# A graph attention block on one core: pair sums merged in the accumulators' bank, the carry row fetched from the stored sums, exponents moved to the front of ScalarE's order, node pieces regrouped, a loop of two turns

## The chip, the cores and the metric

The kernel runs on one core of a Trainium2 chip. The core has five engines that work side by side, each through its own list of instructions: TensorE (PE, with PEld for the weight loads), VectorE (DVE), ScalarE (ACT), GpSimd (POOL) and SyncE (SP, which here only issues DMAs). They meet through semaphores. The metric is the device time in microseconds of one execution.

## The reference

One attention layer over a graph of 6250 nodes and 100,000 edges sorted by destination, then a feed-forward part, residuals and a last layer norm. Cut to what matters here:

```python
q, k, v = feat @ W.T + b            # 6250 x 256 each, 8 heads of 32
score = clip(sum_d(q[dst] * k[src]) / sqrt(32), -10, 10)     # 100000 x 8
ex    = exp(score - segment_max(score, dst)[dst])
den   = segment_sum(ex, dst)
wv    = segment_sum(ex / den[dst] * v[src], dst)
x1    = feat + wv @ Wp.T + bp
h     = gelu(layernorm(x1) * ln_g + ln_b @ W1.T + b1) @ W2.T + b2   # 256 -> 1024 -> 256
out   = layernorm(feat + x1 + h)
```

The clip bounds the exponent, so the kernel leaves the maximum out and divides the sums at the end.

## The kernel before, in words

First the rows k|v of all nodes are computed and stored in DRAM (`kv_rows`), and the first q rows too. Then come the edges. 128 edges make a tile, 4 tiles a batch, 2 batches a pair, 8 batches a turn. There are 196 batches, 98 pairs and 25 turns (0 to 24). Every engine runs its own list over the turns through `turns` (L279): turns 0 to 4 and the last are written out, turns 5 to 23 are a loop (Fori) of one turn. Inside a turn, position i goes from 0 to 7, and n = 8 turn + i is the batch that VectorE begins there.

What a batch costs, engine by engine:

- GpSimd gathers 4 tiles of k|v rows by an indirect DMA each (L313), into one of 8 slots of `kv`. It waits until VectorE has used the slot, and every half turn for a new load of source indices `src_sb` (two buffers, loaded by `load_sources`, L519 of the queue).
- TensorE selects the q rows of the batch's edges from a window of 32 rows for each tile (`q_rows`, L776, into `quad`).
- VectorE multiplies them with k (`products`, L1299), sums by head (`scores`, L1306), clips (L1313), and multiplies v with the exponent of the batch two earlier (`weight`, L1321, into `ev`). Once a pair it makes the one-hot rows (L1287).
- ScalarE makes two exponents of each batch (`exponent`, L1008 into bank 5, L1009 into `ev`), and for each pair the transposed one-hots (L994, L999).
- TensorE sums the weighted rows of a batch by destination into 4 windows of bank 4 (`sums`, L785).

After the second batch of a pair, ScalarE copies bank 4 into `staged` (`stage`, L1017). TensorE then puts the four windows in their places with `place` (L758), and adds the carry: the last node of the pair before may go on in this one, so a second matmul (L762) takes the one row of the previous `acc_sb` that `carry_sel` selects. Both write bank 5, the bank that also holds the exponents. `merge` therefore waits for the exponents, and `weight` of every odd batch waits until `copy_sums` (L1023) has read the result. SyncE stores the 80 rows of sums (`store_sums`, L540) to `agg_rows`.

Nodes ride along in blocks of 256, in `node_steps`. In turn t, block t-1 is loaded (`load_node_sums`, L439), divided by its denominators (`normalise`, i = 3), projected (i = 4, 5), added to x (`residual`, i = 6) and normed (`norm_roots`, i = 7). Block t-2 goes through the feed-forward part: four pieces `ffn1` at i = 1 to 4 with their biases on ScalarE at i = 2 to 5, one Gelu over 128x2048 at i = 5 (L387), and `ffn2` in pieces of 3, 3 and 2 of its 8 slices at i = 6, 7 and 0 of the next turn. Gelu and Exp lie in different tables of ScalarE, so each Gelu has a table load on either side. A unit of q rows is projected each turn as well.

The order on each engine is the order in which the code is written. SyncE's list is in order too: a wait in it holds up every DMA that is written behind it.

An integer check at the start (`check_edges`, `set_flag`) tests that each tile's destinations fit its window, and otherwise a slow general path follows at the end.

## Time and profile before

| | us |
|---|---|
| median of 3 runs | 1251.4 (1251.23 to 1254.77) |
| the profiled execution's own time | 1251.61 |
| its span | 1249.8 |
| first gather issued | 94.84 |
| last gather issued | 1157.58 |
| products of the first and the last batch begin | 103.27, 1175.79 |

The page gives each engine's busy time as a share of the span. PE and DVE both show over 80%. A share does not say which of two such engines sets the pace; the waits and the order in time do. The timeline shows what an engine does at each moment, and in square brackets how long it sat idle before, and what ended that.

### The profile page before, as it was taken

How to read it: one execution, taken by the hardware profiler on the slowest of the kernel's cores; microseconds unless marked ns; L12 is line 12 of the kernel's file. 1: busy time of each engine (PE TensorE's matmuls, PEld its weight loads, DVE VectorE, ACT ScalarE, POOL GpSimd, SP SyncE). 2: the span in 40 equal slices, each digit the busy share in tenths (PEclk: the TensorE clock that was granted, in tenths of full speed). 3: DMA queues.
4: the chain of work that ended last, by engine and by line, in shares of the span. 5: the costliest groups of instructions: out<-in, count | busy, mean ns of one | idle time of the engine just before them, and what ended most of it. 6: DMA issues, size and time to landing. Idle time of an engine off the chain costs nothing.

```text
span 1249.8 us, 24882 instructions
## 1 busy us (share of the span) xinstructions
PE 1032.2 (83%) x6118; PEld 670.4 (54%) x6118; DVE 1014.9 (81%) x1779; ACT 525.6 (42%) x1353; POOL 746.1 (60%) x802
## 2 busy tenths in 40 slices
PE   7893568888988978888888888789889788888887
PEld 6671235555645645555555555456556455555565
DVE  4875788888978978898898888889889888888733
ACT  2221225345444544535445444454444445354332
POOL 0007777777676676767767667666766767667000
PEclk9995588989988988998998988998889889889989
DMA  7777898888888887887887888888788878878210
GB/s 239 247 257 230 284 316 276 251 275 264 254 247 247 265 243 228 268 259 236 258 254 242 256 242 252 255 255 251 238 254 261 246 244 266 248 241 255 69 30 27
DMA packets 158513, 297.71 MB, mean 238 GB/s; under 512 B 34216, under 2 KB 94726, under 8 KB 158471
## 3 DMA queue, kind: packets, MB, share of 16 engines
q0 software_dynamic: 62720, 205.57, 53.4%
q1 hardware_dynamic: 95750, 91.66, 23.2%
q8 instruction: 17, 0.28, 0.1%
q14 instruction: 26, 0.20, 0.1%
HBM read 261.99 MB, written 35.13 MB: 238 GB/s over the span
## 4 chain that ended last, share of the span: by engine, by line
PE 39%; DVE 24%; issue 22%; ACT 8%; POOL 3%; DMA 2%; DVEq 1%; ACTq 1%; POOLq 0%
PE bank L374 10%; DVE score L1306 7%; PE quad L729 5%; DVE ev L1321 5%; PE bank L394 5%; PE bank L758 4%; PE bank L785 4%; POOL kv L313 3%; ACT hid L382 3%; PE bank L762 3%; DVE prod L1299 2%; ACT L1008 2%; PE bank L796 2%; PE quad L776 2%; DVE stats L404 2%
## 5 line engine op out<-in xcount | busy, mean ns | idle before, releaser
L313 POOL DMA_INDIRECT kv<-kv_rows,src_sb x784 | 743.2, 948 | 411.6 <-issue 224.3
L1321 DVE TENSOR_TENSOR ev<-kv,bank 128x1024 f32<-128x1024 f32 x196 | 238.3, 1216 | 93.7 <-ACT ev L1009 71.7
L1299 DVE TENSOR_TENSOR prod<-kv,quad 128x1024 f32<-128x1024 f32 x196 | 238.7, 1218 | 41.5 <-DMA kv<-kv_rows,src_sb 24.1
L1306 DVE TENSOR_REDUCE score<-prod 128x32 f32<-128x1024 f32 x196 | 237.4, 1211 | 0.0
L776 PE MATMUL quad<-qwin,onehotT 32*128 32x256 f32 x1568 | 148.3, 448 | 90.5 <-DVE onehot L1287 73.4
L785 PE MATMUL bank<-ev,onehot 128*32 128x264 f32 x1568 | 144.6, 444 | 86.4 <-DVE ev L1321 85.4
L394 PE MATMUL bank<-w_sb,hid 128*128 128x256 f32 x736 | 202.8, 431 | 0.0
L374 PE MATMUL bank<-hT,w_sb 128*128 128x256 f32 x728 | 176.9, 386 | 0.0
L394 PEld LDWEIGHTS bank<-w_sb,hid 128*128 128x128 f32 x736 | 153.2, 216 | 39.6 <-issue 17.0
L776 PEld LDWEIGHTS quad<-qwin,onehotT 32*128 32x128 f32 x1568 | 66.6, 193 | 164.4 <-issue 110.0
L374 PEld LDWEIGHTS bank<-hT,w_sb 128*128 128x128 f32 x728 | 132.9, 190 | 35.2 <-issue 19.2
L382 ACT ACTIVATE hid<-bank,b_sb 128x256 f32<-128x256 f32 x182 | 76.3, 470 | 119.5 <-PE bank L374 119.5
L785 PEld LDWEIGHTS bank<-ev,onehot 128*32 128x32 f32 x1568 | 32.5, 114 | 161.8 <-DVE ev L1321 120.2
L1023 ACT ACTIVATE acc_sb<-bank 128x264 f32<-128x264 f32 x98 | 38.2, 390 | 187.2 <-PE bank L762 185.1
L758 PE MATMUL bank<-staged,place 128*128 128x264 f32 x196 | 88.1, 539 | 11.4 <-ACT ev L1009 9.0
L1008 ACT ACTIVATE bank<-clipped 128x32 f32<-128x32 f32 x196 | 38.4, 196 | 135.3 <-issue 84.5
L1017 ACT ACTIVATE staged<-bank 128x264 f32<-128x264 f32 x98 | 37.8, 386 | 121.8 <-PE bank L785 118.2
L729 PE MATMUL quad<-wqkv_sb,xT_parts 128*128 128x512 f32 x300 | 71.9, 400 | 13.4 <-DVE xT_parts L1175 13.4
L762 PE MATMUL bank<-acc_sb,carry_sel 128*128 128x264 f32 x194 | 74.1, 471 | 0.0
L758 PEld LDWEIGHTS bank<-staged,place 128*128 128x128 f32 x196 | 36.3, 231 | 69.5 <-ACT ev L1009 50.7
L729 PEld LDWEIGHTS quad<-wqkv_sb,xT_parts 128*128 128x128 f32 x300 | 57.5, 193 | 26.1 <-DVE wqkv_sb L1270 9.2
L999 ACT ACTIVATE onehotT<-distance,one_col 128x256 f32<-128x256 f32 x98 | 49.8, 508 | 9.4
(109 smaller groups left out, 1088.4 us busy)
## 6 DMA issues: line engine op xcount, KB each, us to landing
dst_rows<-edge_dstT SPq DMA_DIRECT2D x200, 64.0 KB
kv_rows<-kv_out SPq DMA_DIRECT2D x25, 512.0 KB, 3.4
...
kv<-kv_rows,src_sb POOLq DMA_INDIRECT x784
...
xT_sb<-xT SPq DMA_DIRECT2D x25, 256.0 KB, 3.8
...
xq_sb<-xT SPq DMA_DIRECT2D x24, 256.0 KB
```

The source lines that it names most:

```text
L313: return nc.gpsimd.indirect_dma_start(out=rows, out_offset=None, in_=kv_dram, in_offset=bass.IndirectOffsetOnAxis(ap=index, axis=0))
L374: last = nc.tensor.matmul(bank[:, j * SB:(j + 1) * SB], w1_sb[:, k * HIDDEN + f * P:k * HIDDEN + (f + 1) * P], hT[:, k], start=(k == 0), s ...
L382: last = nc.scalar.activation(hid[:, f], bank[:, j * SB:(j + 1) * SB], ACT.Identity, bias=b1_sb[:, f:f + 1])
L394: last = nc.tensor.matmul(bank[:, a * C:(a + 1) * C], hid[:, f, a * P:(a + 1) * P], w2_sb[:, f * C:(f + 1) * C], start=False, stop=(a == 1 ...
L729: last = nc.tensor.matmul(rows, lhsT, rhs, start=(n == 0), stop=(n == len(passes) - 1))
L758: last = nc.tensor.matmul(bank5[:, 0:ACC], place[:], staged[:, slot % 2], start=True, stop=not exists(p - 1, PAIRS))
L762: last = nc.tensor.matmul(bank5[:, 0:ACC], carry_sel[:, slot % 2], acc_sb[:, (slot + 3) % 4], start=False, stop=True)
L776: last = nc.tensor.matmul(quad[:, i, 0:C], onehotT[rows, slot // 2, cols], qwin[rows, slot // 2], start=True, stop=True)
L785: last = nc.tensor.matmul(bank4[WIN * i:WIN * (i + 1), 0:ACC], onehot[:, slot // 2, TILES * (slot % 2) + i, :], ev[:, slot % 4, i], start= ...
L1299: nc.vector.tensor_tensor(prod[:, slot % 2].rearrange("p (i c) -> p i c", c=C), kv[:, slot, :, 0:C], quad[:, :, 0:C], ALU.mult).then_inc(s ...
L1306: nc.vector.tensor_reduce(score[:, slot % 2], prod[:, slot % 2].rearrange("p (h d) -> p h d", d=HD), AX.X, ALU.add).then_inc(s_score, 1)
L1321: nc.vector.tensor_tensor(ev[:, slot % 4, :, 0:C].rearrange("p i (h d) -> p i h d", d=HD), kv[:, slot, :, C:2 * C].rearrange("p i (h d) -> ...
```

## The change

Seven things, all in one diff:

1. `merge` writes bank 4, the accumulators' own bank, with one matmul, `place` on `staged`. The second matmul, `carry_sel`, `carry_all` and `select_carry` are gone. The sums of the next pair wait for `copy_sums` (before: for `stage`).
2. The carry row comes in through row 127 of `staged`. A new step `load_carry(p)` on SyncE waits until the sums of pair p-1 are stored (all earlier ones too), reads the pair's base from `bases_sb` and fetches that one row of `agg_rows`. `merge(p)` waits for it. Row 127 of `place` leads to row 0; so a window's last row is given up, and the check asks for one row less (and the fourth window starts at 41).
3. The exponents and the counting row `iota` live alone in bank 5. `weight` no longer waits for `copy_sums`; the one-hots wait for the exponents of the batch before last.
4. On ScalarE `exponent` and `copy_sums` stand first in each position; the Gelu moves from i = 5 to i = 4, behind the exponent.
5. Node pieces move: `ffn1` to i = 0 to 3, `ffn2` to i = 5, 6, 7 in pieces of 3, 2 and 3 slices, the transpose of h to i = 7, `residual` to i = 5, `norm_roots` to i = 6, `output` to 0, `residual_twice` to 1. On VectorE they stand ahead of `scores`, on TensorE ahead of `sums` (but at i = 5).
6. Source indices have 4 buffers and are loaded two turns ahead. The unit of x for q is loaded half a turn earlier. 3 gathers of the empty tail are left out (781 instead of 784).
7. The loop body holds two turns: 6 turns in front, 9 rounds of two, 1 behind.

Two places of the order. First ScalarE, in turn 2, the first with a Gelu; `bank5<-clipped` and `ev<-clipped` are the two exponents of a batch, `hid<-hid` is the Gelu. Before:

```order
L1023 ACTIVATE acc_sb<-bank5 128x264
L1026 ACTIVATE carry_sel<-carry_all 128x1
L336 ACTIVATE wvT<-bank6 128x512
L382 ACTIVATE hid<-bank7,b1_sb 128x256 x2
L387 ACT_TABLE_LOAD
L387 ACTIVATE hid<-hid 128x2048
L1008 ACT_TABLE_LOAD
L1008 ACTIVATE bank5<-clipped 128x32
L1009 ACTIVATE ev<-clipped 128x4x8
```

And now:

```order
L1003 ACTIVATE bank5<-clipped 128x32
L1004 ACTIVATE ev<-clipped 128x4x8
L1018 ACTIVATE acc_sb<-bank4 128x264
L395 ACT_TABLE_LOAD
L395 ACTIVATE hid<-hid 128x2048
L989 ACTIVATE distance<-dst_rows,minus_start 128x256
L994 ACTIVATE onehotT<-distance,one_col 128x256
L1003 ACT_TABLE_LOAD
L1003 ACTIVATE bank5<-clipped 128x32
L1004 ACTIVATE ev<-clipped 128x4x8
```

The Gelu has gone ahead by one position, and an exponent and the copy of the sums stand right in front of it; the transposed one-hots, which before came behind the next exponent, now lie between the Gelu and that exponent.

Second SyncE, written-out turn 4, positions 1 and 2: the store of the sums, the output rows of an older block, a pair's q windows, the load of a block's sums. `TENSOR_LOAD bases_sb` reads a pair's base. Before:

```order
L540 DMA agg_rows<-acc_sb 80x264
L447 DMA out<-y_out 106x256
L499 TENSOR_LOAD bases_sb
L499 ISA x2
L506 ISA
L506 DMA qwin<-q_rows 32x256
...
L439 DMA agg_in<-agg_rows 128x2x264
```

And now, in turn 5, which is written out too:

```order
L555 DMA agg_rows<-acc_sb 80x264
L455 DMA out<-y_out 128x2x256
L508 TENSOR_LOAD bases_sb
L508 ISA x2
L547 ISA
L547 DMA staged<-agg_rows 1x264
L508 TENSOR_LOAD bases_sb
L508 ISA x2
L515 ISA
L515 DMA qwin<-q_rows 32x256
...
L447 DMA agg_in<-agg_rows 128x2x264
```

Between the store and the load of the block's sums there is now another base and another DMA, and the first of them waits for the store to have landed.

```diff
-EX_COL = ACC
-IOTA_COL = C
+EX_COL = 0
+IOTA_COL = 2 * TILES * H
...
         def turns(eng, body):
-            for turn in range(min(5, TURNS - 1)):
-                body(turn)
-            if TURNS > 6:
-                with eng.Fori(5, TURNS - 1) as turn:
-                    body(turn)
-            body(TURNS - 1)
+            looped = max(TURNS - 7, 0) // 2
+            first = 6 if looped else TURNS - 1
+            for turn in range(first):
+                body(turn, turn // 2, turn % 2)
+            if looped:
+                with eng.Fori(3, 3 + looped) as r:
+                    body(2 * r, r, 0)
+                    body(2 * r + 1, r, 1)
+            for turn in range(first + 2 * looped, TURNS):
+                body(turn, turn // 2, turn % 2)
...
-        F2_PARTS = ((0, 1, 2), (3, 4, 5), (6, 7))
+        F2_PARTS = ((0, 1, 2), (3, 4), (5, 6, 7))
...
-                    sp.wait_ge(s_kv[4 * t + b], 64 * (h // 2) if isinstance(h, int) else 64 * h[0])
+                    sp.wait_ge(s_kv[4 * t + b], 64 * (turn + 1))
                 sp.sem_inc(s_gate_sp, 1)
-                col = h * HALF if isinstance(h, int) else h[1]
-                sp.dma_start(src_sb[:, t], edge_src[:, bass.ds(col, HALF)]).then_inc(s_src[t], 16)
+                buffer = 2 * parity + t
+                sp.dma_start(src_sb[:, buffer], edge_src[:, bass.ds((2 * turn + (4 + t)) * HALF, HALF)])\
+                    .then_inc(s_src[buffer], 16)
...
+            def load_carry(p, slot):
+                sp.wait_ge(s_aggst, 16 * p)
+                base = pair_base(p)
+                sp.dma_start(staged[P - 1:P, slot % 2], agg_dram[bass.ds(base, 1), :]).then_inc(s_carry, 16)
 
...
+                    done = 4 * turn + i // 2 - 2
+                    if i == 0 and exists(turn - 1, Q_UNITS - EARLY_Q):
+                        sp.wait_ge(f_qst, 16 * turn)
+                    elif i == 0 and isinstance(turn, int) and turn > 0:
                         sp.wait_ge(f_qst, 16 * (Q_UNITS - EARLY_Q))
-                    if i % 2 == 1 and exists(4 * turn + i // 2 - 2, PAIRS):
-                        store_sums(4 * turn + i // 2 - 2, (i // 2 + 2) % 4)
+                    if i % 2 == 0 and exists(done, PAIRS) and exists(done - 1, PAIRS):
+                        load_carry(done, (i // 2 + 2) % 4)
+                    if i % 2 == 1 and exists(done, PAIRS):
+                        store_sums(done, (i // 2 + 2) % 4)
...
                     if i == 4 and exists(turn, Q_UNITS - EARLY_Q):
                         store_q_unit(turn)
+                    if i == 4 and exists(turn + 1, Q_UNITS - EARLY_Q):
+                        load_q_unit(turn + 1)
...
-                pe.wait_ge(s_exp, min(2 * p + 4, BATCHES) if isinstance(p, int) else 2 * p + 4)
-                last = nc.tensor.matmul(bank5[:, 0:ACC], place[:], staged[:, slot % 2], start=True,
-                                        stop=not exists(p - 1, PAIRS))
                 if exists(p - 1, PAIRS):
-                    pe.wait_ge(s_csel, p)
-                    last = nc.tensor.matmul(bank5[:, 0:ACC], carry_sel[:, slot % 2], acc_sb[:, (slot + 3) % 4],
-                                            start=False, stop=True)
-                last.then_inc(s_mrg, 1)
+                    pe.wait_ge(s_carry, 16 * p)
+                nc.tensor.matmul(bank4[:, 0:ACC], place[:], staged[:, slot % 2], start=True, stop=True)\
+                    .then_inc(s_mrg, 1)
...
-                    if slot % 2 == 1:
-                        pe.wait_ge(s_oh, p + 1)
...
                 if slot % 2 == 0 and exists(p - 1, PAIRS):
-                    pe.wait_ge(s_stc, p)
+                    pe.wait_ge(s_accc, p)
...
+                    if i % 2 == 0 and exists(4 * turn + i // 2 - 2, PAIRS):
+                        merge(4 * turn + i // 2 - 2, (i // 2 + 2) % 4)
+                    if i != 5:
+                        node_steps(turn, i)
                     if exists(n - 2, BATCHES):
                         sums(n - 2, (i - 2) % SLOTS, 4 * turn + (i - 2) // 2)
-                    if i % 2 == 0 and exists(4 * turn + i // 2 - 2, PAIRS):
-                        merge(4 * turn + i // 2 - 2, (i // 2 + 2) % 4)
-                    node_steps(turn, i)
+                    if i == 5:
+                        node_steps(turn, i)
...
+                if i <= 3 and exists(turn - 2, SUPERBLOCKS):
+                    ffn1(turn - 2, i)
+                if i == 1 and exists(turn, Q_UNITS - EARLY_Q):
+                    project_q(turn)
+                if i == 3 and exists(turn - 1, SUPERBLOCKS):
+                    transpose_wv(turn - 1)
                 if i == 4 and exists(turn - 1, SUPERBLOCKS):
-                    transpose_wv(turn - 1)
-                if i == 5 and exists(turn - 1, SUPERBLOCKS):
                     project_out(turn - 1)
-                if i == 0 and exists(turn - 2, SUPERBLOCKS):
-                    transpose_h(turn - 2)
-                if 1 <= i <= 4 and exists(turn - 2, SUPERBLOCKS):
-                    ffn1(turn - 2, i - 1)
-                if i in (6, 7) and exists(turn - 2, SUPERBLOCKS):
-                    ffn2(turn - 2, i - 6)
-                if i == 0 and exists(turn - 3, SUPERBLOCKS):
-                    ffn2(turn - 3, 2)
-                if i == 2 and exists(turn, Q_UNITS - EARLY_Q):
-                    project_q(turn)
+                if i == 7 and not ends and exists(turn - 1, SUPERBLOCKS):
+                    transpose_h(turn - 1)
+                if i >= 5 and not ends and exists(turn - 2, SUPERBLOCKS):
+                    ffn2(turn - 2, i - 5)
...
-                nc.scalar.activation(staged[:, slot % 2], bank4[:, 0:ACC], ACT.Copy).then_inc(s_stc, 1)
+                nc.scalar.activation(staged[0:P - 1, slot % 2], bank4[0:P - 1, 0:ACC], ACT.Copy).then_inc(s_stc, 1)
...
-                nc.scalar.activation(acc_sb[:, slot], bank5[:, 0:ACC], ACT.Copy).then_inc(s_accc, 1)
-
-            def select_carry(p, slot):
-                nc.scalar.activation(carry_sel[:, slot % 2, 0:1], carry_all[:, bass.ds(p, 1)], ACT.Copy)\
-                    .then_inc(s_csel, 1)
+                nc.scalar.activation(acc_sb[:, slot], bank4[:, 0:ACC], ACT.Copy).then_inc(s_accc, 1)
...
-                if i == 5 and exists(turn - 1, SUPERBLOCKS):
+                if i <= 3 and exists(turn - 2, SUPERBLOCKS):
+                    ffn1_bias(turn - 2, i)
+                if i == 3 and exists(turn - 1, SUPERBLOCKS):
                     copy_wv(turn - 1)
-                if i == 0 and exists(turn - 2, SUPERBLOCKS):
-                    norm_out(turn - 2)
-                if i == 1 and exists(turn - 2, SUPERBLOCKS):
-                    scale_h(turn - 2)
-                if 2 <= i <= 5 and exists(turn - 2, SUPERBLOCKS):
-                    ffn1_bias(turn - 2, i - 2)
-                if i == 5 and exists(turn - 2, SUPERBLOCKS):
+                if i == 4 and not ends and exists(turn - 2, SUPERBLOCKS):
                     gelu(turn - 2)
...
+                if i == 7 and not ends and exists(turn - 1, SUPERBLOCKS):
+                    scale_h(turn - 1)
+                if i == 7 and exists(turn - 3, SUPERBLOCKS):
+                    norm_out(turn - 1)
...
                     n = SLOTS * turn + i
+                    if exists(n - 1, BATCHES):
+                        exponent(n - 1, (i - 1) % SLOTS)
+                    if isinstance(turn, int) and n == BATCHES:
+                        gelu(SUPERBLOCKS - 3, range(FC // 2))
+                    done = 4 * turn + i // 2 - 2
+                    if i % 2 == 0 and exists(done, PAIRS):
+                        copy_sums(done, (i // 2 + 2) % 4)
                     node_steps(turn, i)
+                    if i % 2 == 1 and exists(done + 1, PAIRS):
+                        stage(done + 1, (i // 2 + 3) % 4)
+                    if isinstance(turn, int) and n == BATCHES + 1:
+                        gelu(SUPERBLOCKS - 3, range(FC // 2, FC))
                     if i % 2 == 0 and exists(4 * turn + i // 2 + 2, PAIRS):
                         transposed_onehots(4 * turn + i // 2 + 2, (i // 2 + 2) % 4, turn + i // 4 + 1)
-                    if exists(n - 1, BATCHES):
-                        exponent(n - 1, (i - 1) % SLOTS)
-                    p = 4 * turn + i // 2 - 2
-                    if i % 2 == 1 and exists(p + 1, PAIRS):
-                        stage(p + 1, (i // 2 + 3) % 4)
-                    if i % 2 == 0 and exists(p, PAIRS):
-                        copy_sums(p, (i // 2 + 2) % 4)
-                        if exists(p + 1, PAIRS):
-                            select_carry(p + 1, (i // 2 + 3) % 4)
+                    if i == 6 and exists(turn - 1, SUPERBLOCKS):
+                        norm_h(turn - 1)
...
+                if exists(p - 1, PAIRS):
+                    dve.wait_ge(s_exp, 2 * p - 1)
                 if exists(p - 4, PAIRS):
                     dve.wait_ge(s_part, 2 * p - 6)
...
-                    dve.wait_ge(s_accc, p)
                 first = EX_COL + slot % 2 * TILES * H
...
                 inverse_roots(norm_tiles(c), norm_step(c, [2]))
 
             def node_steps(turn, i):
-                if i == 3 and exists(turn, Q_UNITS - EARLY_Q):
+                if i == 0 and exists(turn - 3, SUPERBLOCKS):
+                    output(turn - 3)
+                if i == 1 and exists(turn - 2, SUPERBLOCKS):
+                    residual_twice(turn - 2)
+                if i == 2 and exists(turn, Q_UNITS - EARLY_Q):
                     q_bias(turn)
+                if i == 3 and exists(turn - 1, SUPERBLOCKS):
+                    normalise(turn - 1)
                 if i == 5 and isinstance(turn, int) and turn == 0:
                     split_biases()
-                if i == 3 and exists(turn - 1, SUPERBLOCKS):
-                    normalise(turn - 1)
-                if i == 6 and exists(turn - 1, SUPERBLOCKS):
+                if i == 5 and exists(turn - 1, SUPERBLOCKS):
                     residual(turn - 1)
                     norm_moments(turn - 1)
-                if i == 7 and exists(turn - 1, SUPERBLOCKS):
+                if i == 6 and exists(turn - 1, SUPERBLOCKS):
                     norm_roots(turn - 1)
-                if i == 1 and exists(turn - 3, SUPERBLOCKS):
-                    output(turn - 3)
-                if i == 2 and exists(turn - 2, SUPERBLOCKS):
-                    residual_twice(turn - 2)
-
-            def edges(turn):
+
+            def edges(turn, r, parity):
                 for i in range(SLOTS):
                     n = SLOTS * turn + i
+                    if exists(n - 1, BATCHES):
+                        clip(n - 1, (i - 1) % SLOTS)
                     if exists(n, BATCHES):
                         products(n, i, turn)
                     if i % 2 == 0 and exists(4 * turn + i // 2, PAIRS):
                         onehots(4 * turn + i // 2, i // 2)
                     if exists(n - 2, BATCHES):
-                        weight(n - 2, (i - 2) % SLOTS, 4 * turn + (i - 2) // 2)
+                        weight(n - 2, (i - 2) % SLOTS)
+                    node_steps(turn, i)
                     if exists(n, BATCHES):
                         scores(n, i)
-                    if exists(n, BATCHES):
-                        clip(n, i)
-                    node_steps(turn, i)
-
-            nc.vector.memset(carry_sel[:], 0.0)
+
+            nc.vector.memset(staged[:], 0.0)
             dve.wait_ge(s_iota, 1)
```

## Rows read from the trace of the kernel before

**Rows 1.** The page, part 1: busy time, share of the span, instructions.

```profile
PE 1032.2 (83%) x6118; PEld 670.4 (54%) x6118; DVE 1014.9 (81%) x1779; ACT 525.6 (42%) x1353; POOL 746.1 (60%) x802
```

**Rows 2.** Busy time by stretch (stretch, length, engines, clock, DMA share, GB/s).

```profile
142.00:182.00 40.00, 24.30 (x153) 12.25 (x149) 31.73 (x44) 10.09 (x35) 30.26 (x33) 0.74 0.96 313
...
586.00:1140.00 554.00, 478.67 (x2947) 304.41 (x2949) 481.60 (x808) 260.09 (x680) 378.49 (x400) 0.91 0.82 251
```

**Rows 3.** Waits of VectorE, 182 to 1162 us (total, times, longest).

```profile
DVE ev L1321 <- ACT ev L1009: 71.7, 22, 3.4
DVE ev L1321 <- ACT acc_sb L1023: 13.7, 13, 1.4
```

**Rows 4.** TensorE in order of time: after idling, busy, and near the end.

```profile
631.59 0.88 PE L776 MATMUL quad<-qwin,onehotT 32*128 32x256 f32 x8 [2.55 <-DVE onehot L1287]
...
633.75 1.25 PE L758 MATMUL bank<-staged,place 128*128 128x264 f32 x2
...
1174.57 0.71 PE L758 MATMUL bank<-staged,place 128*128 128x264 f32 x2
...
1196.67 9.81 PE L394 MATMUL quad<-w_sb,hid 128*128 128x256 f32 x32
```

**Rows 5.** VectorE in order of time (start, length, row, idle before).

```profile
187.53 1.22 DVE L1299 TENSOR_TENSOR prod<-kv,quad 128x1024 f32<-128x1024 f32 x1
...
1118.48 1.22 DVE L1299 TENSOR_TENSOR prod<-kv,quad 128x1024 f32<-128x1024 f32 x1 [0.70 <-DVE root L418]
...
1137.06 1.21 DVE L1299 TENSOR_TENSOR prod<-kv,quad 128x1024 f32<-128x1024 f32 x1
...
1138.53 1.21 DVE L1321 TENSOR_TENSOR ev<-kv,bank 128x1024 f32<-128x1024 f32 x1
...
1141.07 1.22 DVE L1299 TENSOR_TENSOR prod<-kv,quad 128x1024 f32<-128x1024 f32 x1
...
1149.60 1.22 DVE L1321 TENSOR_TENSOR ev<-kv,bank 128x1024 f32<-128x1024 f32 x1 [3.24 <-ACT ev L1009]
...
1161.72 1.22 DVE L1299 TENSOR_TENSOR prod<-kv,quad 128x1024 f32<-128x1024 f32 x1 [0.30 <-DVE root L418]
```

**Rows 6.** ScalarE in order of time, around one Gelu.

```profile
612.48 1.28 ACT L387 ACT_TABLE_LOAD   x1
613.77 1.91 ACT L387 ACTIVATE hid<-hid 128x2048 f32<-128x2048 f32 x1
615.70 1.28 ACT L1008 ACT_TABLE_LOAD   x1
```

**Rows 7.** Groups by line (busy, mean ns, idle before): one node piece.

```profile
L400 DVE TENSOR_TENSOR z<-bank,xx 128x512 f32<-128x512 f32 x23 | 15.9, 691 | 9.9 <-PE bank L394 9.0
```

**Rows 8.** GpSimd's 1st and 60th gather, and one after a load of indices.

```profile
94.84 1.10 POOL L313 DMA_INDIRECT kv<-kv_rows,src_sb  x1 [91.04 <-DMA kv_rows<-kv_out]
...
168.75 0.95 POOL L313 DMA_INDIRECT kv<-kv_rows,src_sb  x1 [0.30 <-DVE ev L1321]
...
606.63 0.94 POOL L313 DMA_INDIRECT kv<-kv_rows,src_sb  x1 [2.65 <-DMA src_sb<-edge_src]
```

**Rows 9.** SyncE's queue in order of time, sums stored and fetched.

```profile
194.88 0.33 SPq L540 DMA_DIRECT2D agg_rows<-acc_sb  x1
...
198.29 0.40 SPq L439 DMA_DIRECT2D agg_in<-agg_rows  x1
...
592.36 0.34 SPq L540 DMA_DIRECT2D agg_rows<-acc_sb  x1
...
594.66 1.90 SPq L506 DMA_DIRECT2D qwin<-q_rows  x4
597.03 0.39 SPq L439 DMA_DIRECT2D agg_in<-agg_rows  x1
```

**Rows 10.** DMA issues (KB each, median us to landing).

```profile
wp_sb<-wpT SPq DMA_DIRECT2D x1, 256.0 KB, 4.3
```

**Rows 11.** SyncE's queue: the load of indices before that gather.

```profile
601.80 0.37 SPq L519 DMA_DIRECT2D src_sb<-edge_src  x1
```

164 lines of the change are left out of this document (65 added, 99 removed).

## The prediction

> **What bounds the kernel now.** I read the page's busy shares first, then the stretches, the waits of VectorE, and one turn of it in order of time. The shares leave two candidates, TensorE with 83% and VectorE with 81% [rows 1]. Between 586 and 1140 us VectorE is busy 481.6 of 554 us, and the DMA engines 0.82 of the time [rows 2]. What decides is who waits for whom. From 182 to 1162 us VectorE waits for no matmul worth naming, but 71.7 us (22 times) for exponents and 13.7 us (13 times) for the copy of a pair's sums [rows 3]. TensorE, with its larger share, waits for VectorE's one-hots and products instead, as in the 2.55 us of [rows 4]. So VectorE sets the pace, and its own idle time is what can be won.
>
> The unit is a turn. Turn 2 begins on VectorE at 187.53, turn 24 at 1161.72: 974.2 us for 22 turns, 44.28 us each [rows 5]. In each one the wait for exponents stands once, 3.24 us [rows 5]. Its cause is the block on ScalarE of a table load (1.28), the Gelu (1.91) and a load back (1.28), 4.5 us in one piece, with the next exponent behind it [rows 6].
>
> **The change part by part.**
>
> *Gelu.* It now stands right behind an exponent. I lay out turn time from VectorE's rows. A position with one-hots takes 4.0 us (1137.06 to 1141.07), without them about 3.7, each 0.69 us node piece adds about 0.6 as such rows overlap [rows 5, 7]. From the start of position 4, its `weight` ends at +2.6; ScalarE then has exponents 0.5, copy of sums 0.4, load, Gelu and back 4.5 [rows 6], one-hots about 1.0 in between, exponents 0.5: ready at +9.5. VectorE wants it at position 6 behind the products. Position 4 takes 4.0, position 5 with residual and moments some 6.5, products 1.1: +11.6. Cover of 2 us remains, so the wait goes entirely: -71.7 us. If the cover were gone, each turn would pay what is missing.
>
> ScalarE's table loads are weighed against a rule. The row shows Gelu starting 1.29 us after its load began, and no pause [rows 6]. The Trainium skill (ScalarE: Activation LUTs, What ACT_TABLE_LOAD costs) gives about 2.66 us for a switch, the load and a drain. By that the block would last 7.2 us, the cover would be short by some 0.5 us, and 22 turns would pay 11 us. The trace disagrees, and I go by its rows.
>
> *Merge in bank 4.* `weight` no longer waits for `copy_sums`: -13.7 us [rows 3]. The carry matmul and a small ScalarE instruction go, on engines that wait for VectorE: 0. The sums of the next pair now wait for the copy, about 1 us later than for `stage`; they stand behind a node piece anyway, and TensorE has time: 0.
>
> *Loop of two turns.* Behind a jump back VectorE idles 0.70 us, behind the same row without a jump 0.30 [rows 5]. 18 jumps become 8: -4.0 us.
>
> *Four index buffers.* GpSimd's pace is 73.91 us for 59 steps, 1.25 us per gather, 40.1 us for the 32 of a turn [rows 8]. Today it adds a wait such as 2.65 us twice a turn, because the indices come late; that goes. As GpSimd was ahead of VectorE, it is worth nothing by itself. Without it GpSimd would be the bound at once, since VectorE's turn becomes 44.28 - (71.7 + 13.7 + 4.0) / 22 = 40.2 us. The two are now level. The bytes of a turn, 251 GB/s for 44.28 us, took 35.5 us at the 313 GB/s that stood once [rows 2]; the DMA engines can carry it, at about 0.9 of their time.
>
> *The carry row.* This is the price. Before, SyncE issued the store of the sums at 592.36, the q windows from 594.66 and the load of a block's sums at 597.03, 4.67 us later [rows 9]. Now it first waits until the store has landed (S), reads a base (about 1.0 us, my estimate from the 1.96 us between the store's end and the windows, which also hold an output store), issues the carry row (0.35), and then does windows and load as before (3.4 with their base): S + 4.7. S was never waited for. From above it is at most the 3.4 us between store and load at 194.88 and 198.29, since that load waited for it too [rows 9]; from below nothing excludes 1 us. I take 2.5, nearer to the row. So the block's sums go out 7.2 us behind the store, 2.5 later than now. Their landing (A, 264 KB): 256 KB took 4.3 us to land [rows 10], and 8 KB of indices 4.83 us from issue to the gather behind them [rows 8, 11]. I take 4.5, with ends of 3 and 6 as the DMA engines are busier.
>
> When does VectorE want them? `normalise` now stands at position 3 behind `weight`: 4.6 + 4.3 + 4.6 + 2.3 = 15.8 us into the turn. And when is the store issued? TensorE's position 7 holds q rows, the transposes of h, 12 matmuls of `ffn2` (3 slices where it had 2) and only then the sums; with `stage`, merge, copy and a base read the store comes at about 4.8 us into the turn. But at position 6 VectorE spends 2.7 us in roots, TensorE idles some 3 us, and after such a gap its clock is at the lower level: after 2.55 us idle `place` took 1.25 us against 0.71 [rows 4]. Then it is 6.5 us. The sums are there at 4.8 or 6.5, + 7.2 + 4.5 = 16.5 or 18.2. VectorE waits 0.7 or 2.4 us per turn. I take 1.4, 22 times 1.4 = 31 us given back.
>
> The same S and the landing of the carry row (L) also make a round from merge to merge: merge, copy and signals 1.1, base and issue 1.1, S, base 0.9, L: 3.1 + S + L. With S = 2.5 and L = 3.5 (one row of 1 KB, below the 4.83) it is 9.1 us, four times a turn 36.4, and 1.2 more where SyncE is still busy with other issues: 37.6, beneath 40.2. It is hidden, but not by much.
>
> *Regrouped pieces.* TensorE's list fits under VectorE's in each position at full clock, `residual` finds its projection finished: 0, except for what stands above.
>
> *End.* The last store needs the carry too, which takes back what the earlier last `weight` wins. But block 22 has its Gelu in two halves inside turn 24, so the 9.81 us of `ffn2` that began at 1196.67 [rows 4] begin some 5 us earlier relative to the last products, and all that follows hangs on them: -5 us. Between 0 and -9.
>
> *Sum*, against the profiled execution's own time of 1251.6, which is 0.2 above the median: 1251.6 - 71.7 - 13.7 - 4.0 + 31 - 5 = 1188 us.
>
> **Rivals.**
>
> 1. *No wait for the block's sums.* If S is 2 and A is 3.5, and TensorE keeps its clock, they arrive at 4.8 + 6.7 + 3.5 = 15.0, before 15.8. Then the turn is 40.2 us and the time 1157. For it speaks that nothing before ever waited for this load; against it, that the load moves 2.5 us back while its reader moves forward. The Trainium skill (DMA: Bandwidth & Descriptors, Anatomy of one DMA — SWDGE (gpsimd) path) puts a DMA at a fixed 2.0 us or so plus its bytes over 436 GB/s, which would make S 2.2 and A 2.6, and the result this rival. The 4.83 us for 8 KB here are more than twice that [rows 8, 11], so the rule gets only a share.
>
> 2. *The carry's round becomes the bound, and the kernel slower.* Each pair must wait for a store and a load through DRAM. With S at its upper bound of 3.4 and L at 4.8 the round is 11.3 us, the turn 4 x 11.3 + 1.2 = 46.4, and the time 1251.6 + 22 x 2.1 - 5 = 1293. It decides from S + L = 7.7 on, where the turn passes 44.28; from 7.0 on it exceeds my turn of 41.6. For it: busier DMA engines (0.96 in the stretch of [rows 2]). Against it: a longer turn relieves the DMA engines, and S had its bound at 0.86.
>
> 3. *The general path.* The check asks for one row less, and the fourth window begins at 41. From the reference's own edges the largest place in a window is 29 where 30 are allowed, the smallest 0, and a pair spans at most 70 of 79 nodes. So this one is out.
>
> **How the numbers follow.** My case, a turn of 41.6 us with 1 us to either side, gets 0.63 and reaches from 1166 to 1210. Rival 1 gets 0.22, near 1157. The carry's round gets 0.12: half of it between 1210 and 1248, half slower. The rest is for what I have not seen. What a measurement here can tell from no change is about 0.3%, 4 us. Faster by more than that 0.92, within it 0.02, slower 0.06. The range that should hold the time 8 times in 10 is 1155 to 1224.
>
> **What would show it.** Right: no wait of VectorE for exponents behind a Gelu; none for the copy of the sums; GpSimd's waits for indices gone, and waits for `ev` in their place; a wait of `den` or `wv` for the load of sums, 1 to 2 us once a turn; the last gather near 1090. Rival 1 shows as no such wait and turns of 40.2. Rival 2 shows as waits of the merge for the DMA of `staged`, and behind them waits of VectorE's products for q rows, or of the one-hots for exponents. The forecast fails if S and A lie far from 2.5 and 4.5, or if TensorE falls behind at its lower clock in position 7, which I priced only through the store.

## The result, and the profile after

The changed kernel takes 1259.1 us (median of 7 runs, 1257.3 to 1265.4) against 1252.2 for the kernel before, run beside it (7 runs, 1251.2 to 1255.3): ratio 1.0058, 95% interval 1.0037 to 1.008. It is slower by 0.6%, where 1188 was forecast. The profiled execution took 1265.4 us, its span is 1263.5.

Part 1 of the page and the stretch 586 to 1140 us, the answers to [rows 1, 2]:

```profile
PE 1024.3 (81%) x5924; PEld 655.2 (52%) x5924; DVE 1015.2 (80%) x1777; ACT 518.5 (41%) x1257; POOL 744.0 (59%) x801
```

```profile
586.00:1140.00 554.00, 464.35 (x2755) 290.73 (x2752) 471.78 (x804) 251.57 (x613) 370.27 (x392) 0.86 0.79 245
```

VectorE has as much work as before and does less of it in the stretch; TensorE's granted clock fell from 0.91 to 0.86. VectorE's waits from 182 to 1162 us, as [rows 3] (total, times, longest):

```profile
DVE den L326 <- DMA agg_in<-agg_rows: 77.1, 22, 5.5
DVE x L360 <- PE bank L354: 29.7, 17, 1.9
DVE z L408 <- PE bank L402: 10.2, 14, 2.0
```

The waits for Gelu and for the copy of the sums are gone, 85.4 us. In their place stand 77.1 us for the block's sums, where 31 were forecast, and 29.7 for the projection, where nothing was; 10.2 more stand in front of `z`. One turn shows how. VectorE (start, length, row, idle before; `prod` at 636.76 begins the turn):

```profile
636.76 1.22 DVE L1281 TENSOR_TENSOR prod<-kv,quad 128x1024 f32<-128x1024 f32 x1
...
651.54 1.21 DVE L1301 TENSOR_TENSOR ev<-kv,bank 128x1024 f32<-128x1024 f32 x1
658.28 0.17 DVE L326 TENSOR_SCALAR den<-agg_in 128x16 f32<-128x16 f32 x1 [5.52 <-DMA agg_in<-agg_rows]
```

and SyncE's queue in the same turn, as [rows 9]:

```profile
640.14 1.33 SPq L515 DMA_DIRECT2D qwin<-q_rows  x3
641.74 1.82 SPq L472 DMA_DIRECT2D dst_rows<-edge_dstT  x4
644.55 0.34 SPq L555 DMA_DIRECT2D agg_rows<-acc_sb  x1
645.44 0.42 SPq L455 DMA_DIRECT2D out<-y_out  x1
649.33 0.30 SPq L547 DMA_DIRECT2D staged<-agg_rows  x1
650.79 1.86 SPq L515 DMA_DIRECT2D qwin<-q_rows  x4
653.13 0.40 SPq L447 DMA_DIRECT2D agg_in<-agg_rows  x1
```

The sums that are stored at 644.55 had been copied by ScalarE at 641.36 already:

```profile
641.36 0.39 ACT L1018 ACTIVATE acc_sb<-bank 128x264 f32<-128x264 f32 x1 [0.46 <-PE bank L778]
```

Read the queue backwards. VectorE wants the sums at 652.76. They were asked for at 653.13. Ahead of that stand four windows and a base read (from 649.63 on), the carry row, and the wait for the store to land (from 645.86 to some 648.5). And the store itself is 2.8 us behind the end of the copy, because SyncE was still issuing destination rows.

This last part is not typical. I went through the 20 turns between 190 and 1100 us by the same rows. The store goes out 0.9 to 3.5 us behind the end of the copy, in the middle (median) 1.2, where it was 1.0 before the change. On average the store stands 6.6 us into the turn, the sums are asked for 8.2 us later (7.6 to 8.8), land 5.0 later still, and VectorE, which wants them at 16.4, waits 3.5. So in an ordinary turn it is the wait for the landed store, with what stands behind it in the queue, that makes the sums late. SyncE has no busy share on the page. The chain that ended last, by engine, names it with 15%, and DMAs with 22%:

```profile
PE 29%; DMA 22%; DVE 19%; SPq 15%; issue 12%; POOL 1%; ACT 1%; DVEq 0%; ACTq 0%; POOLq 0%
```

What the prediction said of the other engines is there. ScalarE has the Gelu between its table loads as in [rows 6], and no one waits for the exponents behind it; GpSimd waits for VectorE's `ev` over the whole span, not for indices:

```profile
1164.61 1.28 ACT L395 ACT_TABLE_LOAD   x1
1165.90 1.91 ACT L395 ACTIVATE hid<-hid 128x2048 f32<-128x2048 f32 x1
...
1168.86 1.28 ACT L1003 ACT_TABLE_LOAD   x1
```

```profile
POOL kv L321 <- DVE ev L1301: 112.9, 83, 3.6
```

### The profile page after: what moved, and what is told of

Same layout as the page of the kernel before. It is cut to its first block, busy times and chain, and to the rows that moved or that the text cites. A ratio compares the mean times of both kernels' runs of the same rounds, so it can differ in the third digit from the quotient of the medians.

```text
span 1263.5 us, 24619 instructions
## 1 busy us (share of the span) xinstructions
PE 1024.3 (81%) x5924; PEld 655.2 (52%) x5924; DVE 1015.2 (80%) x1777; ACT 518.5 (41%) x1257; POOL 744.0 (59%) x801
## 4 chain that ended last, share of the span: by engine, by line
PE 29%; DMA 22%; DVE 19%; SPq 15%; issue 12%; POOL 1%; ACT 1%; DVEq 0%; ACTq 0%; POOLq 0%
DMA agg_rows<-acc_sb 12%; DMA agg_in<-agg_rows 6%; SPq L508 5%; PE bank L402 5%; DVE score L1288 5%; PE bank L354 5%; SPq L515 5%; PE quad L748 5%; PE quad L789 4%; DVE prod L1281 3%; PE bank L778 3%; DVE ev L1301 2%; SPq L472 2%; DMA staged<-agg_rows 2%; DVE stats L412 1%
## 5 line engine op out<-in xcount | busy, mean ns | idle before, releaser
L789 PE MATMUL quad<-qwin,onehotT 32*128 32x256 f32 x1568 | 163.4, 490 | 118.0 <-DVE prod L1281 112.6
L402 PE MATMUL bank<-w_sb,hid 128*128 128x256 f32 x736 | 200.2, 428 | 0.0
L789 PEld LDWEIGHTS quad<-qwin,onehotT 32*128 32x128 f32 x1568 | 71.8, 213 | 216.8 <-issue 122.6
L382 PE MATMUL bank<-hT,w_sb 128*128 128x256 f32 x736 | 182.2, 392 | 0.4 <-ACT hid L390 0.4
L402 PEld LDWEIGHTS bank<-w_sb,hid 128*128 128x128 f32 x736 | 157.3, 219 | 30.5 <-issue 5.6
L382 PEld LDWEIGHTS bank<-hT,w_sb 128*128 128x128 f32 x736 | 139.0, 194 | 34.0 <-ACT hid L390 10.3
L390 ACT ACTIVATE hid<-bank,b_sb 128x256 f32<-128x256 f32 x184 | 77.1, 470 | 111.9 <-PE bank L382 111.9
L778 PE MATMUL bank<-staged,place 128*128 128x264 f32 x196 | 84.5, 519 | 44.2 <-DMA staged<-agg_rows 43.4
L354 PE MATMUL bank<-wp_sb,wvT 128*128 128x256 f32 x200 | 82.5, 585 | 0.0
L1012 ACT ACTIVATE staged<-bank 127x264 f32<-127x264 f32 x98 | 38.1, 388 | 107.4 <-PE bank L798 107.2
L326 DVE TENSOR_SCALAR den<-agg_in 128x16 f32<-128x16 f32 x25 | 4.8, 192 | 88.0 <-DMA agg_in<-agg_rows 88.0
## 6 DMA issues: line engine op xcount, KB each, us to landing
agg_rows<-acc_sb SPq DMA_DIRECT2D x98, 82.5 KB
```

The lines of the kernel that those rows point to most:

```text
L354: last = nc.tensor.matmul(bank6[:, a * C:(a + 1) * C], wvT[:, (a * KC + k) * P:(a * KC + k + 1) * P], wp_sb[:, k * C:(k + 1) * C], start=F ...
L382: last = nc.tensor.matmul(bank[:, j * SB:(j + 1) * SB], w1_sb[:, k * HIDDEN + f * P:k * HIDDEN + (f + 1) * P], hT[:, k], start=(k == 0), s ...
L390: last = nc.scalar.activation(hid[:, f], bank[:, j * SB:(j + 1) * SB], ACT.Identity, bias=b1_sb[:, f:f + 1])
L402: last = nc.tensor.matmul(bank[:, a * C:(a + 1) * C], hid[:, f, a * P:(a + 1) * P], w2_sb[:, f * C:(f + 1) * C], start=False, stop=(a == 1 ...
L778: nc.tensor.matmul(bank4[:, 0:ACC], place[:], staged[:, slot % 2], start=True, stop=True)\
L789: last = nc.tensor.matmul(quad[:, i, 0:C], onehotT[rows, slot // 2, cols], qwin[rows, slot // 2], start=True, stop=True)
```

## How I compare the kernels

For each kernel I took the stretch 190 to 1100 us, the length of a turn there (first to last `z` row on VectorE over the turns between), SyncE's waits and the sum of all of VectorE's waits. SyncE's own time is what its waits leave over. For the changed kernel: 20 rows of `z` from 238.2 to 1094.5, so 45.07 us a turn and 20.19 turns in 910 us; its two waits are

```profile
SPq L507 <- DMA agg_rows<-acc_sb: 194.6, 72, 5.5
SPq L552 <- ACT acc_sb L1018: 28.8, 28, 3.7
```

so 9.6 and 1.4 us a turn, and 34.0 are its own. In us, per turn but for the first column:

| kernel | median | turn | SyncE's own | waits for stores | waits for copies | VectorE idle | turn less idle |
|---|---|---|---|---|---|---|---|
| before | 1252.4 | 44.41 | 27.4 | 0.0 | 17.0 | 5.0 | 39.4 |
| changed | 1259.1 | 45.07 | 34.0 | 9.6 | 1.4 | 5.6 | 39.5 |
| e1 sums first | 1228.0 | 43.17 | 33.7 | 9.2 | 0.3 | 3.7 | 39.4 |
| e2 no round | 1264.6 | 45.44 | 33.6 | 10.1 | 1.7 | 6.1 | 39.3 |
| e3 carry by matmul | 1149.3 | 40.26 | 28.3 | 0.1 | 11.8 | 0.9 | 39.4 |
| e5 sums first, no round | 1223.6 | 43.42 | 33.6 | 9.8 | 0.0 | 4.1 | 39.3 |
| e7 windows ahead | 1246.9 | 44.21 | 33.9 | 1.2 | 9.1 | 4.7 | 39.6 |
| e8 bases ahead too | 1201.6 | 42.03 | 34.0 | 0.7 | 7.2 | 2.5 | 39.5 |
| e9 exponent late | 1248.4 | 44.18 | 29.1 | 0.0 | 15.0 | 4.6 | 39.5 |
| e10 wait only | 1186.8 | 41.69 | 27.4 | 10.1 | 4.1 | 2.4 | 39.3 |

The last column is 39.3 to 39.6 in every row: VectorE's own work in a turn is the same in all, and every difference in the turn is its idle time. The columns in the middle show what SyncE does with the turn; what VectorE waits for is told with each run.

## The experiments

**e1, the block's sums first.** In SyncE's `edges`:

```diff
+                    if i == 2 and exists(turn - 1, SUPERBLOCKS):
+                        load_node_sums(turn - 1)
                     if i % 2 == 0 and exists(4 * turn + i // 2 + 2, PAIRS):
                         load_q_windows(4 * turn + i // 2 + 2, (i // 2 + 2) % 4)
...
-                    if i == 2 and exists(turn - 1, SUPERBLOCKS):
-                        load_node_sums(turn - 1)
```

> The changed kernel with one order turned round on SyncE: in each turn the load of the finished block's sums goes out right behind the carry's load, ahead of the four q windows of the same position. Theory A (the block's sums come late because the carry's wait for the store and the q windows stand ahead of them on SyncE, and the rest follows from that wait): in the changed kernel the last window issue stands 1.5 to 3.8 us behind the carry's load and ahead of the sums, so the sums go out about 3 us earlier; VectorE's wait before L326 falls from 3.5 us a turn to under 1, the wait before L360 from 1.8 to under 1, the turn from 45.1 us to 41 to 42, the time to 1160 to 1190 (1175). Theory B (the carry's round of store, load, merge and copy sets the turn): the round is as long as before, the waits move elsewhere, 1255 to 1262. Theory C (the loop of two turns or the regrouped node pieces make the turn longer by themselves): the wait before L326 goes but another takes its place, over 1240.

Measured 1228.0 (1222.0 to 1230.6), ratio to before 0.9816 [0.9789, 0.9843]. Neither number. The wait for the sums fell from 3.5 to 1.1 us a turn, but the turn only by 1.9, for TensorE's list now waits for the carry, 134.8 us where it was 30.6 in the changed kernel (all in 190 to 1100 us):

```profile
PE bank L778 <- DMA staged<-agg_rows: 134.8, 63, 5.0
PE quad L789 <- DVE prod L1281: 22.5, 33, 2.6
```

A pair's round of SyncE in this kernel:

```profile
605.56 0.36 SPq L555 DMA_DIRECT2D agg_rows<-acc_sb  x1
610.54 0.28 SPq L547 DMA_DIRECT2D staged<-agg_rows  x1
612.33 2.26 SPq L515 DMA_DIRECT2D qwin<-q_rows  x4
615.51 0.34 SPq L555 DMA_DIRECT2D agg_rows<-acc_sb  x1
```

The merge ran at 612.54, 2.0 us behind the issue of the row. One round is 9.95 us, the next 11.2 (with destination rows in it), then 9.6.

**e2, the round cut at the merge.**

```diff
-                sp.dma_start(staged[P - 1:P, slot % 2], agg_dram[bass.ds(base, 1), :]).then_inc(s_carry, 16)
+                sp.dma_start(carry_row[P - 1:P, slot % 2], agg_dram[bass.ds(base, 1), :]).then_inc(s_carry, 16)
...
-                if exists(p - 1, PAIRS):
-                    pe.wait_ge(s_carry, 16 * p)
```

> The changed kernel with the carry row loaded into a buffer of its own that nobody reads, and the merge without a wait for it (the sums of a node shared by two pairs are left incomplete; the last row of the staged tile stays zero). SyncE issues and waits exactly as before. Theory A: SyncE's queue is what it was, so the block's sums stay late: 1250 to 1262, with the same 3 us wait before L326. Theory B: the round is cut at the merge, the pairs no longer follow each other through DRAM: 1160 to 1185. Theory C: as A.

1264.6 (1257.7 to 1268.4), ratio 1.0081 [1.0047, 1.0114], for a kernel that leaves the carry out. The round by itself is not what the changed kernel waits for: the rival of a carry round as the bound falls for it.

**e3, the carry as before, all else of the change.**

```diff
-                if exists(p - 1, PAIRS):
-                    pe.wait_ge(s_carry, 16 * p)
-                nc.tensor.matmul(bank4[:, 0:ACC], place[:], staged[:, slot % 2], start=True, stop=True)\
-                    .then_inc(s_mrg, 1)
+                last = nc.tensor.matmul(bank4[:, 0:ACC], place[:], staged[:, slot % 2], start=True,
+                                        stop=not exists(p - 1, PAIRS))
+                if exists(p - 1, PAIRS):
+                    pe.wait_ge(s_csel, p)
+                    last = nc.tensor.matmul(bank4[:, 0:ACC], carry_sel[:, slot % 2], acc_sb[:, (slot + 3) % 4],
+                                            start=False, stop=True)
+                last.then_inc(s_mrg, 1)
```

with `carry_all`, `select_carry` back and `load_carry` gone.

> The changed kernel with the carry as the kernel before has it (selection column and a second matmul from the copied sums, now into bank 4), and no carry load on SyncE; all else of the change stays. Theory A: no wait for a landed store stands ahead of the q windows and the block's sums but the one that the sums themselves need; the sums go out 4.7 us behind the store as before the change, the wait before L326 is 1.4 us or less, the turn 41 to 42 us, the time 1160 to 1190. Theory B: also 1160 to 1190. Theory C: stays over 1240, since loop and regrouping are still there. ScalarE has 97 more copies of a column, some 0.3 us each, beside VectorE's work.

1149.3 (1146.2 to 1150.8), ratio 0.9172 [0.9146, 0.9198]: 8.3% faster than before, and 110 us under the changed kernel. The turn is 40.26 us, the 40.2 that the prediction had worked out for a VectorE that waits for nothing. Its stretch 586 to 1100, and what is left of the wait for the sums:

```profile
586.00:1100.00 514.00, 457.83 (x2994) 301.10 (x2994) 491.46 (x839) 264.76 (x693) 372.24 (x392) 0.96 0.85 267
```

```profile
DVE den L328 <- DMA agg_in<-agg_rows: 0.9, 3, 0.4
```

The queue in one turn of it: 4.5 us from the store to the sums, as before the change, with no wait between them, since the windows' issues fill the time in which the store lands.

```profile
640.58 0.34 SPq L552 DMA_DIRECT2D agg_rows<-acc_sb  x1
641.35 0.41 SPq L457 DMA_DIRECT2D out<-y_out  x1
642.76 1.89 SPq L517 DMA_DIRECT2D qwin<-q_rows  x4
645.08 0.39 SPq L449 DMA_DIRECT2D agg_in<-agg_rows  x1
```

`den` ran at 650.08, 5.0 us later. A load of the sums took 5.15 us in the turn above, and 4.73 in the one before it (608.30 to 613.03), so nearly nothing was to spare. The store stands 6.6 us into the turn on average here, as in the changed kernel; only the way from it to the sums is shorter.

**e4, the loop alone**: the kernel before with 6 turns written out, 9 rounds of two, and the last.

> The kernel before with nothing changed but the loop: six turns written out, nine rounds of two turns, the last turn. The prediction's term: ten loop jumps fewer at 0.4 us, minus 4.0 us: 1248 (1245 to 1251). Theory C (a body of two turns costs by itself): 1256 or more.

1247.0 (12 runs, 1243.2 to 1252.4), ratio 0.9975 [0.9959, 0.9991]: -3.1 us by the ratio, -5.4 by the medians. The term of -4.0 holds.

**e5, e1 and e2 together.**

> The changed kernel with the sums' load right behind the carry's load and with the carry loaded into a buffer that nobody reads (the sums of a node shared by two pairs are left incomplete). Singly, the first edit took the turn from 45.1 to 43.2 us and the second left it (45.4). Theory D (two waits lie one over the other: the late sums, and under them the carry's round of 10 to 11 us a pair): with both gone the turn is VectorE's own 40.3 to 41 us, the time 1149 to 1170. Theory E (what costs is that SyncE stands still for 5 us in each pair, whoever reads the carry): little is won over the 1228 of the sums-first kernel, 1210 to 1230.

1223.6 (1222.6 to 1230.4), ratio 0.9782 [0.9744, 0.982]. Theory D falls, E holds. This kernel leaves the carry out too. Although nobody reads the carry and the sums go out right behind it, VectorE still waits 49.2 us for them. SyncE has one wait left in the stretch, and none for a copy:

```profile
SPq L508 <- DMA agg_rows<-acc_sb: 206.0, 76, 5.1
```

Its own 33.6 us and 9.8 of standing still are 43.4, the whole turn. When it gets to a store, the copy has long been made: the store goes out 5.2 us behind it (median of all stores in the stretch), where that is 1.0 in the kernel before and in e3, and 1.5 in the changed kernel. That is a bound, of an engine whose rows have no busy share on the page. It lies at 43.4 us, so beneath the 45.07 of the changed kernel, and shows once the sums go out earlier.

**e7 and e8, the fetched carry with a better queue.** e7 is e1 with the windows issued ahead of the wait for the store; e8 also reads the pair's base ahead of the waits:

```diff
+                    if i % 2 == 0 and exists(4 * turn + i // 2 + 2, PAIRS):
+                        load_q_windows(4 * turn + i // 2 + 2, (i // 2 + 2) % 4)
                     if i % 2 == 0 and exists(done, PAIRS) and exists(done - 1, PAIRS):
                         load_carry(done, (i // 2 + 2) % 4)
...
+                base = pair_base(p)
                 sp.wait_ge(s_aggst, 16 * p)
-                base = pair_base(p)
```

> The changed kernel (its carry still fetched and used) with SyncE's order at each even position: q windows, then the wait for the store, the carry's load, then the block's sums. In the sums-first kernel a pair's round reads 605.56 store, 610.54 carry, 612.54 merge, 615.51 next store: 9.95 us, of which the last 3.0 hold the merge, the copy and the four windows with their base that SyncE must issue first (612.33 to 614.59). Theory D with SyncE's issues as part of the round: the windows go out while the store is under way, the next store follows the copy, about 1.3 us earlier; the round is 8.6 us, four of them 34.6, below VectorE's 40.3: turn 40.3 to 42, time 1150 to 1190. Theory F (store and load themselves are the round, the windows are beside it): 1220 to 1230 as the sums-first kernel.

> As the kernel with the windows ahead, and the pair's first row is read into its register before the waits of the carry's load and of the store, not behind them. By the gap of 0.7 to 0.8 us from a wait's end to an issue behind a register read, the round gets 1.4 us shorter: where the round still is the bound that is up to 5.6 us a turn, and the time falls below the kernel with the windows ahead; where VectorE is the bound already (theory D there), no difference: within 5 us of it.

e7: 1246.9 (1241.1 to 1256.1), ratio 0.9954 [0.9922, 0.9985]; e8: 1201.6 (1192.8 to 1205.3), 0.9601 [0.9564, 0.9637]. e7 refutes both its numbers: it is slower than e1. SyncE is no longer full (9.1 us of waits for copies), but the carry row now goes out behind windows and a base read, at 5.7 us behind the store instead of 5.0 (605.97 and 611.64 in a turn of it), and TensorE's merge waits with the projection behind it:

```profile
DVE x L360 <- PE bank L354: 67.2, 19, 5.6
DVE den L326 <- DMA agg_in<-agg_rows: 10.9, 13, 1.9
```

In e8 two base reads leave the round, and 2.2 us of the turn go (45 us of time), as its expectation said for a round that is still the bound. So once SyncE has room, the round through DRAM decides; this rests on e8's gain, not on a run that cuts the round in e7's order.

**e9, the exponent put back**, in the kernel of e3:

```diff
-                    if exists(n - 1, BATCHES):
-                        exponent(n - 1, (i - 1) % SLOTS)
...
                     node_steps(turn, i)
+                    if exists(n - 1, BATCHES):
+                        exponent(n - 1, (i - 1) % SLOTS)
```

> The kernel with the carry by matmul (1149 us) with ScalarE's exponent put back behind the copy of the sums and the node pieces of the position, ahead of the staging copy; Gelu stays at position 4. The prediction's step (the wait for Gelu is 3.3 us a turn and goes by ScalarE's order alone): it comes back, 22 times 2.5 to 3.5 us, and the copy's wait of 0.6 a turn with it: 1205 to 1235. Rival (the gain of the 1149 us kernel comes from the bank, the four source buffers or the regrouping): 1149 to 1165.

1248.4 (1242.5 to 1252.5), ratio 0.9961 [0.9941, 0.9981]: 99 us, all but 4 of what e3 had won. The gain needs the exponent's place: without it bank, buffers and regrouping together are worth nothing beyond the loop (e4 takes 1247.0). Whether that place would be enough without the others is not shown (e12, below). The turn grows by 3.92 us, and the prediction had priced the two waits at 85.4 / 22 = 3.9. In the profiled executions (1243.7 and 1150.8) 22 such turns are 86 of 93 us, and 6 more lie behind the last products. The wait is back, in another make-up: 46 times, where the kernel before had 20 for 65.2 us and 13 for the copy in the same stretch.

```profile
DVE ev L1309 <- ACT ev L1002: 87.4, 46, 3.4
```

**e10 to e13, wait and load apart.** In the kernel of e3, e10 adds only the wait (below), e11 only a base read and a row of `kv_rows` into a buffer that nobody reads, and e13 is e10 with the block's sums right behind the wait. e12 is e4 with the exponent first, as e9's diff turned round.

```diff
+                    if i % 2 == 0 and exists(done, PAIRS) and exists(done - 1, PAIRS):
+                        sp.sem_inc(s_gate_sp, 1)
+                        sp.wait_ge(s_aggst, 16 * done)
```

> The kernel with the carry by matmul (1149 us) with only the wait of the fetched carry added on SyncE: at each even position it waits until the last store of sums has landed, and loads nothing. Reckoned from the windows 190 to 1100 us, SyncE's own work is 28.3 us a turn there and 33.6 to 34.0 in all kernels that fetch a row, and its waits for landed stores 9.5 us. Theory P (SyncE's time per turn is what counts: own work plus waits for landed stores over VectorE's 40.3): 28.3 + 9.5 = 37.8, below 40.3, so no cost: 1149 to 1165. Theory S (the wait stands ahead of the block's sums, which then go out 8 us behind the store and not 4.5, and VectorE has only 0.3 us to spare there: den at 650.08, issue at 645.08, 4.7 for the load): 3.3 us a turn, 1149 + 22 x 3.3 = 1222 (1210 to 1240).

> The kernel with the carry by matmul with only the carry's load added on SyncE, without a wait: a register read and one row of the key and value table per pair into a buffer that nobody reads, ahead of the q windows. Theory P: 28.3 + 5.5 = 33.8 us of SyncE a turn, no cost: 1149 to 1158. Theory S: the block's sums go out up to 1.5 us later where 0.3 is to spare: up to 1.2 us a turn, 1165 to 1178.

> As the kernel with the wait only, and the block's sums go out right behind that wait, ahead of the q windows. Theory P: as without the wait, 1149 to 1165. Theory S: the sums go out 5.0 + 0.3 us behind the store where 4.5 were: 0.5 us of wait a turn, 1149 + 22 x 0.5 = 1160 (1150 to 1172), which lies 50 us or more under the kernel with the wait only.

> The kernel before with two edits of the change alone: the loop of two turns (1247 us by itself) and on ScalarE the exponent at the head of each position, ahead of the node pieces. Carry, banks, source buffers and pieces are the old ones. The prediction's step: the wait for Gelu (3.3 us a turn) goes, that for the copy of the sums (0.6 a turn) stays since banks and copy are the old ones: 1247 - 22 x 3.3 = 1174 (1165 to 1190). Rival (the freed exponent collides with what shares bank 5, or Gelu's 4.5 us only move to the next position): 1225 to 1247.

All four came out on a chip on which the kernel before takes 1834 us, and the four run again on another, where it takes 1846. There e10, e11 and e13 took 1587, 1601 and 1587 us (again 1588, 1596, 1590) and e12 1803 (1813, and 1793 beside 1859 on a third such chip). In ratios, e10, e11 and e13 are at 0.863 to 0.875, e12 at 0.984, 0.988 and 0.969. VectorE waits there for something the trace does not name, in front of its products (e13, 300 to 1400 us):

```profile
DVE prod L1293 <- remote: 252.7, 65, 6.1
```

Those runs don't tell the theories apart: VectorE's longest wait is another one, and e10, e11 and e13 lie within 1% of each other. e11, e12 and e13 therefore stay open for a chip on which the kernel before takes 1252 us. The runs do show that on the slower chips the other parts of the change count. In e12, which has the old two index buffers, GpSimd waits for indices as below (whole span); in e10, with four, it has no such wait. The kernel before had 88.9 us of it on a chip of 1252 us.

```profile
POOL kv L315 <- DMA src_sb<-edge_src: 518.7, 46, 16.3
```

No run changes the buffers alone, so that they make the difference between 0.87 and 0.97 to 0.99 there is likely and not shown.

Only e10 was run once more beside a kernel before of 1251.2 us: 1186.8 (three runs, 1182.2 to 1192.6; a fourth took 1209.9), ratio 0.9491 [0.9432, 0.9551]. That is 38 us over e3 by the medians and 40 by the ratios, between P (1149 to 1165) and S (1210 to 1240). SyncE has 4.1 us of waits for copies left, so it is not full; theory P, which had no cost for that case, is refuted. The mechanism is S's, with less than its size:

```profile
DVE den L328 <- DMA agg_in<-agg_rows: 32.0, 22, 2.7
```

1.5 us a turn, of the 1.43 by which the turn grew. The sums go out 6.45 us behind the store (655.58 and 662.03), 1.95 later than in e3's turn; in the middle of all turns 6.8 and 4.5, so 2.3 later, where I had put 3.5. So the wait for a landed store alone costs 40 us. With the base read and the load of the row behind it, and no other engine waiting for that row, it is e2 (which also lacks the carry's second matmul), at 1264.6: another 75 us or more. The sums go out 8.4 us behind the store there. Of the 3.75 us that the turn grows from e10 to e2, 2.0 are VectorE's wait for the sums (69.6 us in the stretch) and 1.5 its wait for the projection (35.3 us, in e10 5.7).

## Why the prediction was wrong

*Gelu, merge, loop.* Right in this kernel, where the parts stand together. The waits are gone, and e3 runs at the floor of 40.2 us; the Gelu block is 4.5 us and hidden. Alone, e4 confirms the loop. Gelu's and the copy's price per turn holds too (e9), as a sum.

*Four index buffers.* Right as a fact: GpSimd waits for `ev` now (112.9 us over the span) and for no indices. The last gather is issued at 1170.11, not near 1090, as all turns are longer. The page counts 782 gathers where the kernel before has 784: two are left out, not three. "Worth nothing by itself" was not run.

*The carry row.* This step failed: its price of 1.4 us a turn was 3.5. Of the chain that gives it, store, sums issued, sums landed, every term was too short. From the store to the sums it said S + 4.7, with S = 2.5. In the turn above it is 8.58 us: 3.80 from the carry's issue to the sums (the price said 3.75), and 4.78 before it, which without the base read of some 0.9 makes S 3.9. That is also the median of the 72 waits of SyncE for a landed store in the stretch, which reach from 2.4 to 5.9. The upper bound of 3.4 came from one early pair, whose store took 3.2 to land; it bounds no other pair, and the share of the DMA engines does not order them: 0.86 there, 0.79 in the stretch 586 to 1100 of the changed kernel. Late in the program, with the gathers over, the same step is short:

```profile
1212.72 0.34 SPq L555 DMA_DIRECT2D agg_rows<-acc_sb  x1
1214.71 0.39 SPq L447 DMA_DIRECT2D agg_in<-agg_rows  x1
```

The sum, with the forecast's middle beside the average of the 20 turns, in us:

| | forecast | measured |
|---|---|---|
| store issued, into the turn | 4.8 or 6.5 (5.65) | 6.6 |
| from the store to the sums | 7.2 | 8.2 |
| the load (A) | 4.5 | 5.0 |
| VectorE wants them | 15.8 | 16.4 |
| wait | 1.4 | 3.5 |

So S is the largest miss, the store's time and the load come next, and the later reader takes 0.6 back. The 4.8 was too early, whoever fetches the carry: in e3 too the store stands 6.6 us into the turn on average. (The reading that `ffn2` has three slices in position 7 "where it had 2" is a slip; it had three there before as well.) The turn shown above is one of the worst, with its store at 7.8 and a wait of 5.5.

There is a second error, which the first one hides in this kernel. I let SyncE issue the store when the sums were copied, and never added up its turn. Its 27.4 us of own time were no concern before. The carry adds 6.6 and makes it stand still for 9.6, together 43.6, while VectorE could turn in 40.3. With the sums issued earlier that is what holds the kernel at 1224 (e5), so even an S of the right size in my sum would not have told what a better order wins.

Of the 45.07 us, 40.26 are e3's turn, 3.5 the wait for the sums and 1.4 that for the projection. The forecast had 1.4 for both; its turn of 41.6 is short by 3.5 us, 22 times that are 77, and the profiled execution came out 77 us above the forecast. That the two agree so closely is partly luck, as the end and the loop have their own small differences.

*TensorE's clock* was named as what would make the forecast fail, and priced only through the store. It made `residual` late instead, and that is the second term that failed: the prediction put it at nothing ("`residual` finds its projection finished: 0"), and it was 1.4 us a turn. Projections of three turns of the changed kernel, and the transposes of the same block ahead of them:

```profile
481.99 0.66 PE L339 MATMUL bank<-ident,wv 128*128 128x128 f32 x4 [0.46 <-DVE wv L332]
486.26 1.99 PE L354 MATMUL bank<-wp_sb,wvT 128*128 128x256 f32 x8
```

```profile
436.69 0.66 PE L339 MATMUL bank<-ident,wv 128*128 128x128 f32 x4 [2.24 <-DVE wv L332]
442.31 3.78 PE L354 MATMUL bank<-wp_sb,wvT 128*128 128x256 f32 x8
```

```profile
526.37 0.66 PE L339 MATMUL bank<-ident,wv 128*128 128x128 f32 x4 [2.24 <-DVE wv L332]
530.64 1.99 PE L354 MATMUL bank<-wp_sb,wvT 128*128 128x256 f32 x8
```

The eight matmuls take 1.99 us at the higher level of the clock (1.00 granted from 486.26 to 488.25, so 2.4 GHz) and 3.78 at the lower (0.50 from 442.31 to 446.09, 1.2 GHz). In the second of the turns shown VectorE waited 1.80 us for them, in the others not. The idle time for `wv` does not decide in a single turn: it was 2.24 us in the slow one and in the third, fast one. Over the kernels the link is plain. In the kernel before, in e3 and in e9 all projections of the stretch take 1.99 or 2.00 us; in e10, where VectorE waits 1.5 us for the sums, 20 of 22 do; in the changed kernel, with 3.5, 4 of 20; in e2 none. In e7 the sums come nearly in time, but TensorE idles for the carry row instead, 92.5 us in the stretch, and 2 of 21 are fast. So in most turns the wait for the sums is paid twice: once itself, and once as the lower of TensorE's two clock levels in the projection of the same block.

*The end.* From the last products (1196.15) to the end of the span it is 67.4 us, against 74.0: -6.6 for -5 forecast.

*The rivals.* The wait for nothing (1157) is what e3 does, without the fetched row. The round as the bound, "and slower": its S + L = 7.7 was not reached. In the turn of e1 above it is 7.0 us from the store to the merge (605.56 to 612.54); some 0.9 of that are the base read, which leaves 6.1 for S + L. The changed kernel is slower for another reason, and cutting the round wins nothing in e2, and 4 us in e5 against e1. But the round lies closely beneath: e7 and e8 meet it, by what e8 wins. No rival had SyncE's own turn as a bound, which e5 meets.
